# VectorE sums the first weights after the last count is in the plane

## The reference

```
L0: graph attention, 8 heads, selu
L1: three times  agg = segment_sum(x[src], dst); x = relu(relu((x+agg) @ wa + ba) @ wb + bb)
L2: graph attention, 4 heads, skip product, layernorm
L3: three times  norm = dinv[row] * ew * dinv[col]; x = segment_sum(xw[row] * norm, col) + b
```

## Time and profile before

| | us |
|---|---|
| three executions | 6221.3, 6223.53, 6226.63 |
| median | 6223.53 |
| profiled execution, its own time | 6229.74 |
| its span, first to last instruction | 6227.3 |
| mean granted clock of TensorE | 0.772 |

### The profile page before, as it was taken

One profiled execution on the slowest core, in us unless ns is written; L12 is line 12 of the kernel. 1 busy time (PEld: TensorE's weight loads), 2 busy tenths in 40 slices (PEclk: granted clock), 3 DMA queues, 4 the chain that ended last, 5 costly groups with the idle time before them and its releaser, 6 DMA issues. The chain is left out here.

```text
span 6227.3 us, 42910 instructions
## 1 busy us (share of the span) xinstructions
PE 3499.0 (56%) x13009; PEld 2056.1 (33%) x13009; DVE 2950.2 (47%) x6265; ACT 1693.3 (27%) x1995; POOL 3313.5 (53%) x3349
## 2 busy tenths in 40 slices
PE   3000000050097889999997111111089999999999
PEld 2000000010053347777785110000044445444444
DVE  4766666768666754565554355555571000000111
ACT  2433334021001015666675123333240000000000
POOL 5777777577777777777771777777620000000000
PEclk7555555565598999999998555555589999999999
DMA  4565565499854343344575233333368888888887
GB/s 146 190 231 209 209 221 194 124 371 365 316 165 122 117 122 112 112 121 126 158 249 185 82 114 110 121 110 121 126 215 274 295 296 294 291 295 299 291 302 260
DMA packets 508282, 1255.61 MB, mean 202 GB/s; under 512 B 114543, under 2 KB 163157, under 8 KB 499349
## 3 DMA queue, kind: packets, MB, share of 16 engines
q1 hardware_dynamic: 387076, 1126.44, 53.1%
q0 software_dynamic: 119952, 125.65, 8.1%
q10 hardware_dynamic: 1024, 0.79, 0.1%
HBM read 873.83 MB, written 378.71 MB: 201 GB/s over the span
## 5 line engine op out<-in xcount | busy, mean ns | idle before, releaser
L817 POOL DMA_INDIRECT plane<-total,cell x1568 | 1621.9, 1034 | 489.6 <-issue 423.4
L450 POOL DMA_INDIRECT gb<-rows,src x1564 | 1490.5, 953 | 524.9 <-issue 475.5
L993 PE MATMUL psum<-gb,big 128*128 128x512 f32 (+1 forms) x3822 | 1585.5, 569 | 3.1 <-DVE turned L1173 2.6
L993 PEld LDWEIGHTS psum<-gb,big 128*128 128x128 f32 x3822 | 693.8, 191 | 767.0 <-issue 766.0
L1382 PE MATMUL psum<-gb,row_part 128*128 128x512 f16 x1911 | 421.4, 374 | 475.1 <-DMA gb<-plane 475.1
L2284 ACT COPY gb<-turned 128x1632 f32<-128x1632 f32 (+3 forms) x138 | 450.8, 3267 | 722.3 <-DVE turned L2377 722.3
L1382 PE MATMUL psum<-strips,ring 128*128 128x512 f32 (+1 forms) x2548 | 610.0, 394 | 13.5 <-issue 7.5
L2304 PE MATMUL psum<-identity,end_top 128*8 128x128 f32 (+1 forms) x2 | 0.8, 375 | 1085.2 <-DVE end_top L2383 1085.2
L1402 ACT CAST strips<-gb 128x1024 fp32r<-128x1024 f16 (+1 forms) x529 | 558.9, 1075 | 109.7 <-PE psum L1388 38.0
L2733 PE MATMUL psum<-w_L_gnn_skip_W,turned 128*128 128x128 f32 x98 | 39.0, 501 | 891.5 <-ACT turned L2751 891.5
L2377 DVE TENSOR_TENSOR_SCAN turned<-gb,psum 128x1632 f32<-128x1632 f32 (+3 forms) x138 | 457.8, 3317 | 68.3 <-ACT gb L2266 65.8
(11 more groups left out here) (414 smaller groups left out, 4651.3 us busy)
## 6 DMA issues: line engine op xcount, KB each, us to landing
gb<-plane SPq DMA_DIRECT2D x588, 512.0 KB, 4.5
gb<-plane SPq DMA_DIRECT2D x294, 576.0 KB, 4.7
plane<-turned SPq DMA_DIRECT2D x49, 3200.0 KB, 28.3
gb<-plane SPq DMA_DIRECT2D x588, 256.0 KB, 3.1
gb<-plane SPq DMA_DIRECT2D x294, 288.0 KB, 3.3
plane<-turned SPq DMA_DIRECT2D x49, 1600.0 KB, 10.9
runs<-gb SPq DMA_DIRECT2D x33, 1748.0 KB, 6.1
runs<-gb SPq DMA_DIRECT2D x33, 1610.0 KB, 5.7
```

What stands on the lines that cost most here:

```text
L450: m.s_rows[b % BUFS].up(nc.gpsimd.indirect_dma_start(m.batch(b, columns, row)[:, j, 0:width], None, table, bass.IndirectOffsetOnAxis(ap=m. ...
L817: done.up(m.nc.gpsimd.indirect_dma_start(plane, bass.IndirectOffsetOnAxis(ap=m.cell[:, r:r + 1], axis=0), total[:, r:r + 1], None), 16)
L993: mm = nc.tensor.matmul(m.psum[:, self.bank(r, 0, i), 0:nodes], rows, slot[:, a:a + nodes], start=(s == 0), stop=False)
```

## The change

VectorE waits for `s_epoch` = 8 before it starts on the first 196 weights: until every count has landed in plane 0. Nothing else is edited.

```diff
         def _(dve):
             selu.dve(dve, Count(m, dve, m.rooms, m.room_products, m.step_bank.bitcast(bf16)))
             count = Count(m, dve, m.junk, m.products)
+            dve.wait_ge(m.s_epoch.sem, EPOCHS)
             count.weigh(0, 2 * EACH)
             weighed = 2 * EACH
```

## The result

| | before | after |
|---|---|---|
| median of 18 executions, us | 6224.73 | 6234.72 |
| lowest to highest | 6221.3 to 6226.73 | 6231.96 to 6240.51 |
| profiled execution, its own time | 6229.74 | 6232.73 |
| its span | 6227.3 | 6230.6 |

The account below looks back on a forecast made before the run. GpSimd was taken to bound up to 2230 us, TensorE from 2321 us. TensorE's second layer 9.4 us later (the 11.0 gain included) plus 1.0 for the clock gave +10.4 us, 6233.9 us; range 6224.5 to 6242.

Parts of the forecast that it names:

- The gain, 11.0 us: 60 GpSimd scatters beside VectorE's first weights fall to 0.97 us each, so the first layer's last round ends 11.0 us sooner.
- The inference of the Trainium skill: VectorE instructions with two SBUF inputs do not stall GpSimd's descriptor generation; by that the gain would be 0.
- Rival 1: The scatters' surplus before the last epoch's end is not VectorE's doing and stays: 6244.9 us, chance 0.09.
- The loss, 113.1 us of weights behind the last epoch: VectorE's 196 weights, 113.1 us, start only at 2216.7, so TensorE's second layer starts 9.4 us later than now.
- The clock, 1.0 us: A longer TensorE idle gap before the second layer lowers its granted clock: 1.3 us more at most, 1.0 taken.
- rival 3: Idle time or faster steps in TensorE's second layer give back some 8 of the 10 us: 6226 us, chance 0.10.
- the prediction's own sign: Rival 3 holds if TensorE's second-layer start to the third layer's end gets shorter by more than 2 us.
- GpSimd's end, no part: GpSimd's end in plane 1 moves by +1.9 us with a slack of 81 us, so it adds nothing.
- The term for the first scatter of plane 1: GpSimd's first plane 1 scatter waits for VectorE's first weight, counted as 1.9 us more.
- Rival 2: VectorE finishes the 196 weights within 92.7 us, before the second layer wants it: whole gain kept, 6212.5 us, chance 0.08.

Follow-up runs that it names:

- psum_no_wait: Kernel before, no wait, second input of the first 196 weight instructions in PSUM instead of SBUF (sums not true): 6213.37 us against 6225.02, 11.7 us faster.
- half_wait: Changed kernel with only 98 weights behind the wait, the other 98 handed out in the later layers' loop: 6216.22 us against 6225.02 for the kernel before.
- psum_wait: Changed kernel, wait kept, second input of the first 196 weight instructions in PSUM (sums not true): 6234.63 us against 6225.02 for the kernel before.
- half_no_wait: Kernel before, no wait, 98 weights up front and the other 98 in the loop; repeat on another chip: 6227.63 us against 6227.71.
- wait_after_60: Changed kernel with the wait moved behind the first 60 of the 196 weights: 6215.03 us against 6225.02 for the kernel before, 10.0 us faster.
- wait_after_25: Changed kernel with the wait behind the first 25 weights: 7192.33 us against 7181.12 for before on the slow chip; repeated elsewhere, 6230.44 against 6227.71.

## Why the prediction was right

Its steps, against the trace of after and the runs:

- *The gain, 11.0 us.* Measured 11.2 at epoch eight, 11.7 as a time by itself (psum_no_wait). The cause named was right too: with the second input in PSUM there is no surplus. A part was missed: the gap ahead of the last round shrank from 25.31 to 14.12 us, the prediction counted nothing for the clock there, and the round became 1.3 us shorter. With VectorE late this changes nothing in the sum; in psum_no_wait and half_wait it shows, as they start the second layer 11.9 and 12.2 us sooner.
- *The inference of the Trainium skill* in "SBUF — State Buffer", section "Who interferes with whom", that a VectorE `tensor_tensor` with both inputs in SBUF does not stall descriptor generation, does not hold for the scatters here. L718 is such a `TENSOR_TENSOR`, and the scatter beside it took 1.61 us in the trace of before (at 2139.05) and 1.50 in that of psum_wait (at 2271.33), with 0.97 on either side of the latter. It is not so each time: in psum_no_wait two scatters beside L718 took 0.97 and 1.05 us (at 2135.04 and 2192.35). Of L794, 61 scatters take 58.2 us beside the instructions with one SBUF input, and 60 take 69.3 with two. Rival 1, which rested on the inference, is out. The rule ahead of it, that two SBUF inputs contend with a GpSimd instruction that reads SBUF, may well be what is seen: each scatter is given its rows by `cell`, which lies in SBUF. No run here takes that read away.
- *The loss, 113.1 us of weights behind the last epoch.* Measured 113.2, and TensorE's second layer started 9.1 us later, released by `DVE ring L1417`, in place of 9.4. The handover from VectorE to TensorE took 0.75 us (2322.58 to 2323.33) where 0.92 were put in.
- *The clock, 1.0 us.* Not shown. The low level did come behind the gap of 26.09 us (0.60 over the first 6 us of the second layer, 0.72 before). But behind gaps of 4.46 to 4.49 us the same 6 us had 0.50 in psum_no_wait, 0.50 in half_wait, 0.51 in half_no_wait and 0.74 in wait_after_60. So in these traces the length of the gap does not decide it, and the term is smaller than what changes from run to run.
- *Nothing gives it back (rival 3).* Right: 9.1 us at the second layer's start, 10.0 in the median. By the prediction's own sign the way from there to the end of the third layer would have to be over 2 us shorter; it is 3.7 us longer (1065.3 and 1061.6), where the forecast had 1.0.
- *GpSimd's end, no part.* Right, shown by psum_wait, where its surplus is gone and the time stays. Its size was off: -1.2 us measured, +1.9 forecast. The term for the first scatter of plane 1 has a slip as well, as its parts give 2.0 + 0.2 + 0.15 - 0.7 = 1.65 and not 1.9; measured it is 2.5 (3.19 - 0.70). Why the rest came out shorter is open.
- *Rival 2* did not come true, as the 196 weights took 113.2 us. Its condition, that VectorE's stretch behind the wait is under 92.7 us, is what wait_after_60 makes: 87.0 us of VectorE's work left, and 10.0 us faster than before. The bound lies where it was put or close to it: with 87.0 us left there is no loss, with 104.5 us (25 weights ahead) TensorE waits 17.75 us for VectorE, 13.3 more than for ScalarE, which would put the bound at about 91 us.

The mechanism was right in both large terms, each within 0.3 us. That the sum came out within 0.4 us of the median is in part luck: the interval of the median is 8 us wide, the term for the clock is not shown, and the two traces are 12.8 us apart at the end of the third layer. The range of the forecast itself, 6 to 15 us, was set by feeling for single rows.

## What to carry to other kernels

When a wait keeps one engine out of another's way, the work does not vanish, it moves: work out what the held engine still has to do from the release on, and compare it with what the next to want it has (here 113 us against 93). If it is too long, put the wait inside the work, so that what is left just fits; 60 of 196 items ahead turned 10 us lost into 10 us gained, for the same wait. The other way is to take the contention away and not the overlap (here an operand in PSUM). In psum_no_wait that was worth 11.7 us, not clear of the 10.0 by these intervals. Its 196 columns don't hold the true sums, though; whether the weights can lie in PSUM is not shown.

## What the runs showed of the hardware

A scatter of GpSimd (an indirect DMA) takes 0.97 us beside an idle VectorE, and as much beside instructions of 1.0 us whose second input is in PSUM (L731, and L795 in psum_no_wait). Beside L794, of 1.0 us and with both inputs in SBUF, it takes up to 1.6 us in that stretch. The surplus goes with the length of VectorE's instruction: in the whole trace of before, scatters beside L794 alone average 0.99 us below 56 elements and 1.37 from 672 on, but not evenly between (1.21 from 392 to 447, 1.09 from 504 to 559). VectorE was not seen to slow down for it. Its 196 weights took 113.1 us beside scatters of plane 0 and 1, 113.2 beside those of plane 1 alone, with no gap above 0.21 us, and L718 took 0.97 us beside the scatter of 1.61 and 0.98 with GpSimd idle (at 2209.37 in the trace of after). L794 itself was hardly ever seen without scatters.

One input in SBUF is not always harmless. In the trace of before a cast of VectorE from f16 to fp32r, 1024 elements in 0.69 us, has a scatter of 1.40 us beside it (12 scatters beside this cast average 1.11):

```profile
3253.82 1.40 POOL L817 DMA_INDIRECT plane<-total,cell  x1 [0.30 <-issue]
...
3253.68 0.69 DVE L1400 CAST strips<-gb 128x1024 fp32r<-128x1024 f16 x1 [1.00 <-PE psum L1382]
```

One chip took 7181 us for the kernel before. On it an epoch of the counts took 131 us (2284.11 to 2415.13 us in the trace of wait_after_25) and not 116 (2000.90 to 2117.04 in the trace of before), and GpSimd waited 558 us in all for VectorE's weights, 289 of them in one piece (before: 52.2 us, at most 0.3 in one piece):

```profile
PEld psum L1382 <- issue: 1006.4, 460, 380.1
...
POOL plane L817 <- DVE passing L794: 557.8, 187, 288.7
```

TensorE's weight loads (first row) had waits there for which the profile names no releaser, 1006 us in place of 433 in the trace of before. Why that chip is slow is open. With intervals of 24 to 28 us, a difference of 10 us could not be told on it.
